# Routing-table entries loaded into registers four at a time instead of one by one

## The chip, the cores and the metric

The kernel runs on one core of one Trainium2 chip. The metric is the device time of one execution in microseconds (us); before the change it is 420.66 us, the median of three runs (418.88, 420.66 and 421.48). Engines are named as in the profile: PE (TensorE), DVE (VectorE), ACT (ScalarE), POOL (GpSimd) and SP (SyncE, which here only issues DMA transfers).

## The reference

One block of a vision transformer with a mixture of experts, in float32, on 32 images of 37 tokens of width 256 (1184 tokens):

```python
h = patches @ W.T + b + pos_embd                     # 36 patches an image, and a class token
h = h + attention(layernorm(h))                      # 16 heads, silu on q and k, rope, causal, gated
x = layernorm(h)
topidx = 6 of 32 experts, from 2 of 4 groups, by sigmoid(x @ gate.T) + bias
routed = sum over the 6 of  w_e * (silu(x @ w_gate[e]) * (x @ w_up[e])) @ w_down[e]     # hidden 128
shared = (silu(x @ sg) * (x @ su)) @ sd
anchor = the same form with 1 of 16 anchor experts, chosen by topidx[:, 0] // 2          # hidden 64
h = h + routed + shared + 0.1 * anchor
```

Which expert a token goes to is known only once the gate has been computed, on the chip.

## The kernel before, in words

The first half (up to about 195 us) embeds the patches, does attention tile by tile, normalises again, computes the gate and, per token, its place in each expert's list. POOL scatters every token's row (width, weights and target rows, 322 numbers) into lists in HBM (`rows_d`), one list an expert, seven copies a token.

The second half goes over 112 tiles of 128 rows of these lists, called visits here: 25 for the anchor experts (kind "A", `FIRST_ROUTED` = 25) and 87 for the routed ones, of kinds "F" (a full tile of one expert), "M" and "X" (tiles at the seams of the lists). The kinds stand fixed in the program. Which expert's weights a visit takes, and from which row on, depends on the data: DVE computes it as a table of four lines of integers in the first partition of `scratch`, one column a visit. Line 0 is the place of the expert's weights in the weight tile `W`, line 1 the first row in `rows_d`, line 2 the column with the expert's weight, line 3 the place of the sum tile. An engine that needs an entry loads it into a register (`entry`, line 319, a TENSOR_LOAD in its instruction queue) and uses the register in an address:

- SP, `load_rows` (lines 405 to 414): waits until the row buffer is free (six buffers), loads the row number (line 1), issues the transfer of 128 rows into `G`.
- ACT, `copy_up` (line 977): loads the weights' place (line 0) and copies the expert's up and gate weights to `UPW`; then copies the turned rows (`turned_copy`, line 985) and does the silu (`hidden_silu`, line 990).
- PE: for visit i it loads the weights' place of visit i-1 (line 0, `down_weights`), then multiplies the turned rows with the up weights (line 823), turns the rows of visit i+2 (line 812) and multiplies the hidden values of visit i-1 with its down weights (line 838).
- DVE, main loop: loads the column of visit i+2 (`columns`, line 2) and, where the tile is summed and not of kind "M", the sum tile's place (line 3), then forms the hidden product of visit i (line 1597), takes weights and target rows of visit i+2 (lines 1566 and 1574, or 1576 for kind "F"), and adds the result of visit i-1 to its sum tile (`accumulate`, line 1589).

So an anchored visit has two loads on DVE and one on each of SP, ACT and PE. All instruction streams are written out in full, in the order given; engines wait for each other through semaphores only. POOL sends finished tiles to HBM, and at the end (from about 374 us) SP reads the sums back and DVE adds them to `h`.

Of the kernel before, what the change touches and what calls it, by code (L numbers as in the profile page):

```python
# [24 lines left out]
P = 128  # L25
D = 256
# [30 lines left out]
ANCHOR_COLS = ANCHORS * ANCHOR_WX  # L57
# [24 lines left out]
GB = 6  # L82
# [3 lines left out]
def routed(i):  # L86
    return KINDS[i] != "A"
# [22 lines left out]


FIRST_ROUTED = ANCHOR_TILES
EARLY_COLS = 19482
TRI4 = 3 * LISTS
SMALL = TRI4 + 23
PIECES = [[(0, 4), (4, 8), (8, NT)]] * (CHOICES - 1) + [[(0, 4), (4, 7), (7, 9), (9, 10), (10, NT)]]
assert KINDS.count("F") == FULL and KINDS.count("M") == MIXED and KINDS.count("X") == EXTRAS
assert all(KINDS[:i].count("X") >= min(EXTRAS, INDEX[i] + 1) for i in range(XT) if KINDS[i] == "M")
assert FULL * D <= ANCHOR_COLS and XT <= P
LATE_PIECES = 10  # L120
BIG = 3.0e38

# [1 line left out]
def build(nc, pt, wt, posr, brow, wqkv, wo, wg1, wg2, lnwb, gwt, gbias, sgu, sd, wx,  # L124
          ident_c, cmask_c, turn_c, parity_c, cs_c, before_c, small_c, out):
    with ExitStack() as ctx:
# [187 lines left out]
        fin_ok, out_st = sem("fin_ok"), sem("out_st")  # L314
        block = ctx.enter_context(nc.Block())

        def entry(engine, q, i, top):

            return nc.values_load(table[0:1, q, bass.ds(i, 1)], engines=(engine,), min_val=0, max_val=top,  # L319
                                  skip_runtime_bounds_check_because="the table is computed within these bounds")  # L320

        def patch_view(b):

# [25 lines left out]
        def _(sp):  # L349
# [52 lines left out]
            sp.wait_ge(table_ok, 1)  # L402
            sp.wait_ge(av_ps, NT)

            def load_rows(i):
                if i == FIRST_ROUTED:
                    sp.wait_ge(scat, 16 * NT * TOPK)
                if i >= GB:

                    sp.wait_ge(T_ps, i - GB + 1)  # L410
                    sp.wait_ge(meta_ok, i - GB + 1)
                row = entry(mybir.EngineType.SP, 1, i, DUMMY_ROW + P)
                sp.dma_start(G[:, i % GB, :], rows_d[bass.ds(row, P), :]).then_inc(g_ld[i % GB], 16)

            def load_part(c):

# [85 lines left out]
        def _(pe):  # L502
# [301 lines left out]
            pe.wait_ge(table_ok, 1)  # L804
            pe.wait_ge(valid_ok, 1)
            pe.wait_ge(hs_ok, NB - 2)

            def turn_rows(i):

# [16 lines left out]

            def down_weights(i):
                size, at = (WX, UP_COLS) if routed(i) else (ANCHOR_WX, ANCHOR_UP_COLS)
                e = entry(mybir.EngineType.PE, 0, i, (W_COLS if routed(i) else ANCHOR_COLS) - size)
                return W[:, bass.ds(e, size)][:, at:at + D]  # L830

            def down(i, weights):
                if i == FIRST_ROUTED:
# [19 lines left out]
        def _(act):  # L853
# [120 lines left out]
            for b in range(3, NB):  # L974
                shared_silu(b)

            def copy_up(i):

                size, n = (WX, UP_COLS) if routed(i) else (ANCHOR_WX, ANCHOR_UP_COLS)
                e = entry(mybir.EngineType.Activation, 0, i, (W_COLS if routed(i) else ANCHOR_COLS) - size)  # L980
                act.copy(UPW[:, i % 2, 0:n], W[:, bass.ds(e, size)][:, 0:n]).then_inc(upw_ok, 1)  # L981

            def turned_copy(i):
                act.wait_ge(T_ps, i + 1)
# [31 lines left out]
        def _(dve):  # L1016
# [524 lines left out]
            dve.wait_ge(table_ok, 1)  # L1541
            dve.wait_ge(valid_ok, 1)

            def sum_tile(i):
                if KINDS[i] == "M":
                    k = INDEX[i] * RING
                    return mixed[:, k:k + D], mixed_rows[:, k + D:k + RING]
                top = (MIXED if routed(i) else ANCHOR_PACKED) * RING - RING
                k = entry(mybir.EngineType.DVE, 3, i, top)
                sums, rows = (mixed, mixed_rows) if routed(i) else (ring, ring_rows)  # L1550
                return sums[:, bass.ds(k, D)], rows[:, bass.ds(k + D, 1)]

# [1 line left out]

            def columns(i):

                at = entry(mybir.EngineType.DVE, 2, i, ALPHA_COL)
                if summed(i):
                    tiles[i] = sum_tile(i)
                return at  # L1560

            def take_columns(i, at):

                mask = valid[:, i:i + 1]
                dve.wait_ge(T_ps, i + 1)
                dve.tensor_tensor(wcol[:, i:i + 1], G[:, i % GB, bass.ds(at, 1)], mask, ALU.mult)  # L1566
                to = G[:, i % GB, TO_ROW:ROW][:, bass.ds(at, 1)]
                if summed(i):
                    if KINDS[i] != "A" and INDEX[i] == 0:
                        dve.wait_ge(mixed_zero, 2)  # L1570
                    if i > 0:
                        dve.wait_ge(meta_ok, i)
                    rows = tiles[i][1]
                    dve.scalar_tensor_tensor(rows, to, mask, rows, ALU.mult, ALU.add).then_inc(meta_ok, 1)  # L1574
                else:
                    dve.tensor_copy(tok_full[:, INDEX[i]:INDEX[i] + 1], to).then_inc(meta_ok, 1)
# [92 lines left out]
def constants():  # L1669
# [16 lines left out]
    small[:, 2 * LISTS:3 * LISTS] = P + np.arange(LISTS) * LIST_ROWS  # L1686
    small[:, TRI4:TRI4 + 16] = np.tril(np.ones((GROUPS, GROUPS)), -1).ravel()
    small[:, TRI4 + 16] = row
    number = np.array([number_of(i) if i < XT else -1 for i in row], np.float32)
    small[:, TRI4 + 17] = number  # L1690
    small[:, TRI4 + 18] = [0 if i >= XT or KINDS[i] == "X" else -P * number[i] for i in row]
    last = np.array([ANCHOR_PACKED - 1 if i < XT and KINDS[i] == "A" else MIXED - 1 for i in row], np.float32)
    small[:, TRI4 + 19] = [(number[i] if i < XT and KINDS[i] == "A" else 0) - last[i] for i in row]
    small[:, TRI4 + 21] = last
    small[:, TRI4 + 20] = SPARE_ROW + row
    small[:, TRI4 + 22] = [ANCHOR_COLS if i < XT and KINDS[i] != "A" else 0 for i in row]
    return dict(ident_c=np.eye(P, dtype=np.float32), cmask_c=causal, turn_c=turn, parity_c=parity, cs_c=cs.astype(np.float32),
                before_c=before, small_c=small)

# [16 lines left out]
```

## Time and profile before

| what | before |
|---|---|
| runs | 418.88, 420.66, 421.48 us; median 420.66 us |
| span of the profiled execution, first to last instruction | 412.1 us |
| time around the span, by the three runs | 6.8 to 9.4 us |
| PE busy | 343.3 us (83%) |
| DVE busy | 278.0 us (67%) |
| ACT busy | 190.0 us (46%) |
| POOL busy | 181.7 us (44%) |

The profile records one execution; its own time from outside is not given, its span is. Register, branch and semaphore instructions and the loads from the table do not count as busy: they show as waits put down to "issue", or in an engine's queue, which the views name DVEq, SPq, ACTq or PEldq (PEld is PE's weight load). "PEclk" is the clock granted to PE as a share of its full speed. The chain of waits is followed back from the last instruction to what released it.

### The profile page before, as it was taken

How to read it: one execution, taken by the hardware profiler on the slowest of the kernel's cores; microseconds unless marked ns; L12 is line 12 of the kernel's file. 1: busy time of each engine (PE TensorE's matmuls, PEld its weight loads, DVE VectorE, ACT ScalarE, POOL GpSimd, SP SyncE). 2: the span in 40 equal slices, each digit the busy share in tenths (PEclk: the TensorE clock that was granted, in tenths of full speed). 3: DMA queues.
4: the chain of work that ended last, by engine and by line, in shares of the span. 5: the costliest groups of instructions: out<-in, count | busy, mean ns of one | idle time of the engine just before them, and what ended most of it. 6: DMA issues, size and time to landing. Idle time of an engine off the chain costs nothing.

```text
span 412.1 us, 8817 instructions
## 1 busy us (share of the span) xinstructions
PE 343.3 (83%) x2552; PEld 299.1 (73%) x2552; DVE 278.0 (67%) x1171; ACT 190.0 (46%) x471; POOL 181.7 (44%) x159
## 2 busy tenths in 40 slices
PE   5999999999899968773889999999999999994000
PEld 3786978779687857561677789999999999993000
DVE  0466789989798886798357775555565665666675
ACT  1152153441545233400157777777877777771000
POOL 6000000588888768767871374344422344433000
PEclk9999999999999997985989999999999999998555
DMA  7999999986698643694555576555555559531998
GB/s 234 298 335 335 329 341 328 420 320 119 123 337 252 126 96 86 218 387 137 152 162 130 167 214 180 162 158 165 165 145 162 166 155 291 168 113 58 303 303 245
DMA packets 55823, 88.44 MB, mean 215 GB/s; under 512 B 16145, under 2 KB 46521, under 8 KB 55513
## 3 DMA queue, kind: packets, MB, share of 16 engines
q1 hardware_dynamic: 38192, 67.66, 52.9%
q0 software_dynamic: 16720, 19.48, 17.8%
q10 hardware_dynamic: 864, 0.73, 0.6%
q8 instruction: 21, 0.34, 0.3%
q14 instruction: 26, 0.21, 0.2%
HBM read 50.62 MB, written 37.09 MB: 213 GB/s over the span
## 4 chain that ended last, share of the span: by engine, by line
PE 60%; DVE 20%; DMA 8%; issue 3%; ACT 3%; SPq 3%; DVEq 2%; POOLq 0%
PE B L823 20%; PE B L838 10%; PE B L514 6%; PE B L812 5%; DMA W<-sums_d 4%; PE B L549 4%; PE B L632 3%; PE B L598 2%; PE B L618 2%; DVEq L319 2%; DMA e_sb<-rows_d 2%; SPq L419 2%; DVE ring L1589 1%; PE B L656 1%; DMA W<-in_pt 1%
## 5 line engine op out<-in xcount | busy, mean ns | idle before, releaser
L457 POOL DMA_INDIRECT rows_d<-spent,slot x77 | 104.1, 1352 | 97.3 <-issue 90.9
L823 PEld LDWEIGHTS B<-e_sb,UPW 128*128 128x128 f32 x796 | 105.4, 193 | 10.7 <-issue 5.5
L823 PE MATMUL B<-e_sb,UPW 128*128 128x128 f32 x796 | 108.9, 278 | 1.5 <-issue 1.5
L1597 DVE TENSOR_TENSOR e_sb<-e_sb,B 128x128 f32<-128x128 f32 (+1 forms) x112 | 32.3, 288 | 62.2 <-ACT e_sb L990 55.8
L981 ACT COPY UPW<-W 128x512 f32 (+1 forms) x112 | 63.9, 570 | 22.2 <-issue 13.9
L838 PE MATMUL B<-W,e_sb 128*128 x224 | 69.3, 391 | 0.8 <-DVE e_sb L1597 0.8
L483 POOL DMA_INDIRECT sums_d<-spent x32 | 31.1, 972 | 48.7 <-DVE spent L1589 47.9
L812 PE MATMUL B<-ident,e_sb 128*128 128x128 f32 x224 | 43.1, 274 | 1.9 <-DMA e_sb<-rows_d 1.8
L990 ACT ACTIVATE e_sb<-B 128x128 f32<-128x128 f32 (+1 forms) x112 | 30.9, 276 | 22.2 <-PE B L823 20.8
L514 PE MATMUL B<-W 128*111 128x256 f32 (+1 forms) x132 | 34.2, 406 | 4.6 <-DMA W<-in_pt 4.5
L483 POOL DMA_INDIRECT sums_d<-W,tok_full x24 | 23.2, 966 | 30.3 <-ACT W L995 29.7
L838 PEld LDWEIGHTS B<-W,e_sb 128*128 128x128 f32 x224 | 34.0, 192 | 3.5 <-issue 1.7
L985 ACT COPY e_sb<-B 128x256 f32<-128x256 f32 x88 | 32.3, 367 | 4.6 <-PE B L812 4.6
L514 PEld LDWEIGHTS B<-W 128*111 128x111 f32 (+1 forms) x132 | 23.3, 184 | 12.2 <-DMA W<-in_pt 5.3
L1589 DVE SCALAR_TENSOR_TENSOR spent<-B,wcol,spent 128x256 f32<-128x256 f32 (+1 forms) x63 | 30.4, 482 | 1.7 <-DVE spent L1574 0.8
L812 PEld LDWEIGHTS B<-ident,e_sb 128*128 128x128 f32 x224 | 28.5, 144 | 2.3 <-DMA e_sb<-rows_d 2.1
L1626 DVE TENSOR_TENSOR h<-h,W 112x1024 f32<-112x1024 f32 (+3 forms) x23 | 23.2, 1047 | 8.4 <-DMA W<-sums_d 8.4
L1289 DVE TENSOR_TENSOR e_sb<-B,spent 111x444 f32<-111x444 f32 (+1 forms) x44 | 23.6, 597 | 4.1 <-PE B L598 4.1
L1566 DVE TENSOR_TENSOR wcol<-e_sb,turn 128x1 f32<-128x1 f32 x112 | 17.2, 153 | 4.0 <-PE B L812 3.8
L598 PE MATMUL B<-W 32*111 32x222 f32 (+1 forms) x176 | 15.5, 369 | 4.8 <-ACT W L909 4.8
L549 PE MATMUL B<-W 128*128 128x222 f32 (+1 forms) x96 | 18.1, 341 | 0.6 <-ACT W L886 0.6
L606 PE MATMUL B<-spent 128*128 128x256 f32 x70 | 18.6, 414 | 0.0
(250 smaller groups left out, 524.0 us busy)
## 6 DMA issues: line engine op xcount, KB each, us to landing
e_sb<-rows_d SPq DMA_DIRECT2D x112, 161.0 KB, 2.3
rows_d<-spent SPq DMA_DIRECT2D x2, 7728.0 KB, 44.4
W<-in_wx SPq DMA_DIRECT2D x1, 6643.0 KB
W<-sums_d SPq DMA_DIRECT2D x13, 448.0 KB, 9.4
W<-in_wx SPq DMA_DIRECT2D x10, 516.5 KB, 9.5
W<-in_wx SPq DMA_DIRECT2D x1, 4576.0 KB, 18.7
W<-in_pt SPq DMA_DIRECT2D x4, 666.0 KB, 6.9
W<-sums_d SPq DMA_DIRECT2D x7, 336.0 KB, 11.1
```

The costliest lines, as they stand in the source:

```text
L457: pool.indirect_dma_start(rows_d, bass.IndirectOffsetOnAxis(ap=slot[0:n, t, j:j + 1], axis=0), xrow[0:n, t, :], None).then_inc(done, 16)
L483: pool.indirect_dma_start(sums_d, bass.IndirectOffsetOnAxis(ap=rows, axis=0), src, None).then_inc(done, 16)
L514: m = pe.matmul(B[0][0:TILES[t], i * D:(i + 1) * D], patch_view(b)[:, c, at:at + TILES[t]], w_patch[:, c, :], start=c == 0, stop=c == PC - 1)
L549: m = pe.matmul(B[4 + half][:, c * BT:c * BT + n], w_qkv[:, k, lo:lo + P], xnT[:, k, 0:n], start=k == 0, stop=k == KC - 1)
L812: m = pe.transpose(B[i % 2][:, k * P:(k + 1) * P], G[:, i % GB, k * P:(k + 1) * P], ident[:, :])
L823: mm = pe.matmul(B[2 + i % 2][:, m * P:(m + 1) * P], UPW[:, i % 2, at:at + P], GT[:, i % 2, k, :], start=k == 0, stop=k == KC - 1)
L838: pe.matmul(B[6 + i % 2][:, 0:D], hid[:, i % 2, :], weights, start=True, stop=True).then_inc(D_ps, 1)
L981: act.copy(UPW[:, i % 2, 0:n], W[:, bass.ds(e, size)][:, 0:n]).then_inc(upw_ok, 1)
L985: act.copy(GT[:, i % 2, :, :].rearrange("p k s -> p (k s)"), B[i % 2][:, 0:D]).then_inc(gt_by[True], 1)
L990: act.activation(S[0:n, i % 2, :], B[2 + i % 2][0:n, 0:P], ACT.Silu).then_inc(silu_ok, 1)
L1589: dve.scalar_tensor_tensor(sums, B[6 + i % 2][:, 0:D], wcol[:, i:i + 1], sums, ALU.mult, ALU.add).then_inc(acc_ok, 1)
L1597: dve.tensor_tensor(out[0:n, i % 2, :], S[0:n, i % 2, :], ups, ALU.mult).then_inc(H_ok, 1)
```

## The change

`entry` is replaced by `entries`: one load instruction fetches up to four neighbouring entries of a line into up to four registers, and a dictionary on each engine keeps them for the visits that follow. A group does not go beyond the anchored visits or the end, and starts where the column number is a multiple of four; for that, the routed visits' columns are moved to begin at column 28 in place of 25 (`place_of`), in the table, in the constants from which it is computed, and in the column of `valid`. On SP a group's load comes before the waits for the row buffer, in place of behind them.

```diff
--- before.py
+++ after.py
@@ -110,13 +110,20 @@
 FIRST_ROUTED = ANCHOR_TILES
+
+
+def place_of(i):
+
+    return i if i < FIRST_ROUTED else i - FIRST_ROUTED - (-FIRST_ROUTED // 4) * 4
+
+
 EARLY_COLS = 19482
 TRI4 = 3 * LISTS
 SMALL = TRI4 + 23
 PIECES = [[(0, 4), (4, 8), (8, NT)]] * (CHOICES - 1) + [[(0, 4), (4, 7), (7, 9), (9, 10), (10, NT)]]
 assert KINDS.count("F") == FULL and KINDS.count("M") == MIXED and KINDS.count("X") == EXTRAS
 assert all(KINDS[:i].count("X") >= min(EXTRAS, INDEX[i] + 1) for i in range(XT) if KINDS[i] == "M")
-assert FULL * D <= ANCHOR_COLS and XT <= P
+assert FULL * D <= ANCHOR_COLS and place_of(XT - 1) < P
 LATE_PIECES = 10
 BIG = 3.0e38
 
@@ -314,10 +321,17 @@
         fin_ok, out_st = sem("fin_ok"), sem("out_st")
         block = ctx.enter_context(nc.Block())
 
-        def entry(engine, q, i, top):
-
-            return nc.values_load(table[0:1, q, bass.ds(i, 1)], engines=(engine,), min_val=0, max_val=top,
-                                  skip_runtime_bounds_check_because="the table is computed within these bounds")
+        def entries(engine, q, i, top):
+
+            at = place_of(i)
+            n = 4 - at % 4
+            if i < FIRST_ROUTED:
+                n = min(n, FIRST_ROUTED - i)
+            n = min(n, XT - i)
+            _, found = nc.values_load_multi_w_load_instructions(
+                table[0:1, q, at:at + n], engines=(engine,), min_val=0, max_val=top,
+                skip_runtime_bounds_check_because="the table is computed within these bounds")
+            return {i + k: v for k, v in enumerate(found)}
 
         def patch_view(b):
 
@@ -402,15 +416,18 @@
             sp.wait_ge(table_ok, 1)
             sp.wait_ge(av_ps, NT)
 
+            row_of = {}
+
             def load_rows(i):
+                if i not in row_of:
+                    row_of.update(entries(mybir.EngineType.SP, 1, i, DUMMY_ROW + P))
                 if i == FIRST_ROUTED:
                     sp.wait_ge(scat, 16 * NT * TOPK)
                 if i >= GB:
 
                     sp.wait_ge(T_ps, i - GB + 1)
                     sp.wait_ge(meta_ok, i - GB + 1)
-                row = entry(mybir.EngineType.SP, 1, i, DUMMY_ROW + P)
-                sp.dma_start(G[:, i % GB, :], rows_d[bass.ds(row, P), :]).then_inc(g_ld[i % GB], 16)
+                sp.dma_start(G[:, i % GB, :], rows_d[bass.ds(row_of[i], P), :]).then_inc(g_ld[i % GB], 16)
 
             def load_part(c):
 
@@ -804,6 +821,7 @@
             pe.wait_ge(table_ok, 1)
             pe.wait_ge(valid_ok, 1)
             pe.wait_ge(hs_ok, NB - 2)
+            weights_of = {}
 
             def turn_rows(i):
 
@@ -826,8 +844,9 @@
 
             def down_weights(i):
                 size, at = (WX, UP_COLS) if routed(i) else (ANCHOR_WX, ANCHOR_UP_COLS)
-                e = entry(mybir.EngineType.PE, 0, i, (W_COLS if routed(i) else ANCHOR_COLS) - size)
-                return W[:, bass.ds(e, size)][:, at:at + D]
+                if i not in weights_of:
+                    weights_of.update(entries(mybir.EngineType.PE, 0, i, (W_COLS if routed(i) else ANCHOR_COLS) - size))
+                return W[:, bass.ds(weights_of[i], size)][:, at:at + D]
 
             def down(i, weights):
                 if i == FIRST_ROUTED:
@@ -974,11 +993,14 @@
             for b in range(3, NB):
                 shared_silu(b)
 
+            weights_of = {}
+
             def copy_up(i):
 
                 size, n = (WX, UP_COLS) if routed(i) else (ANCHOR_WX, ANCHOR_UP_COLS)
-                e = entry(mybir.EngineType.Activation, 0, i, (W_COLS if routed(i) else ANCHOR_COLS) - size)
-                act.copy(UPW[:, i % 2, 0:n], W[:, bass.ds(e, size)][:, 0:n]).then_inc(upw_ok, 1)
+                if i not in weights_of:
+                    weights_of.update(entries(mybir.EngineType.Activation, 0, i, (W_COLS if routed(i) else ANCHOR_COLS) - size))
+                act.copy(UPW[:, i % 2, 0:n], W[:, bass.ds(weights_of[i], size)][:, 0:n]).then_inc(upw_ok, 1)
 
             def turned_copy(i):
                 act.wait_ge(T_ps, i + 1)
@@ -1541,12 +1563,16 @@
             dve.wait_ge(table_ok, 1)
             dve.wait_ge(valid_ok, 1)
 
+            sum_at, column_at = {}, {}
+
             def sum_tile(i):
                 if KINDS[i] == "M":
                     k = INDEX[i] * RING
                     return mixed[:, k:k + D], mixed_rows[:, k + D:k + RING]
                 top = (MIXED if routed(i) else ANCHOR_PACKED) * RING - RING
-                k = entry(mybir.EngineType.DVE, 3, i, top)
+                if i not in sum_at:
+                    sum_at.update(entries(mybir.EngineType.DVE, 3, i, top))
+                k = sum_at[i]
                 sums, rows = (mixed, mixed_rows) if routed(i) else (ring, ring_rows)
                 return sums[:, bass.ds(k, D)], rows[:, bass.ds(k + D, 1)]
 
@@ -1554,14 +1580,15 @@
 
             def columns(i):
 
-                at = entry(mybir.EngineType.DVE, 2, i, ALPHA_COL)
+                if i not in column_at:
+                    column_at.update(entries(mybir.EngineType.DVE, 2, i, ALPHA_COL))
                 if summed(i):
                     tiles[i] = sum_tile(i)
-                return at
+                return column_at[i]
 
             def take_columns(i, at):
 
-                mask = valid[:, i:i + 1]
+                mask = valid[:, place_of(i):place_of(i) + 1]
                 dve.wait_ge(T_ps, i + 1)
                 dve.tensor_tensor(wcol[:, i:i + 1], G[:, i % GB, bass.ds(at, 1)], mask, ALU.mult)
                 to = G[:, i % GB, TO_ROW:ROW][:, bass.ds(at, 1)]
@@ -1686,14 +1713,16 @@
     small[:, 2 * LISTS:3 * LISTS] = P + np.arange(LISTS) * LIST_ROWS
     small[:, TRI4:TRI4 + 16] = np.tril(np.ones((GROUPS, GROUPS)), -1).ravel()
     small[:, TRI4 + 16] = row
-    number = np.array([number_of(i) if i < XT else -1 for i in row], np.float32)
-    small[:, TRI4 + 17] = number
-    small[:, TRI4 + 18] = [0 if i >= XT or KINDS[i] == "X" else -P * number[i] for i in row]
-    last = np.array([ANCHOR_PACKED - 1 if i < XT and KINDS[i] == "A" else MIXED - 1 for i in row], np.float32)
-    small[:, TRI4 + 19] = [(number[i] if i < XT and KINDS[i] == "A" else 0) - last[i] for i in row]
-    small[:, TRI4 + 21] = last
+    small[:, TRI4 + 17] = -1
+    for i in range(XT):
+        k, anchor = place_of(i), KINDS[i] == "A"
+        last = (ANCHOR_PACKED if anchor else MIXED) - 1
+        small[k, TRI4 + 17] = number_of(i)
+        small[k, TRI4 + 18] = 0 if KINDS[i] == "X" else -P * number_of(i)
+        small[k, TRI4 + 19] = (number_of(i) if anchor else 0) - last
+        small[k, TRI4 + 21] = last
+        small[k, TRI4 + 22] = 0 if anchor else ANCHOR_COLS
     small[:, TRI4 + 20] = SPARE_ROW + row
-    small[:, TRI4 + 22] = [ANCHOR_COLS if i < XT and KINDS[i] != "A" else 0 for i in row]
     return dict(ident_c=np.eye(P, dtype=np.float32), cmask_c=causal, turn_c=turn, parity_c=parity, cs_c=cs.astype(np.float32),
                 before_c=before, small_c=small)
 
```

Two places show what the engines execute. The first is the start of the visits on SP, where the rows of the first tiles are fetched; TENSOR_LOAD is the load from the table (`scratch`), ISA the register arithmetic of the address, DMA the transfer of 128 rows into `G` (which lies in `e_sb`). Before:

```order
L319 TENSOR_LOAD scratch [waits table_ok,av_ps,ini_d,scat_anchor]
L413 ISA
L413 DMA e_sb<-rows_d 128x322
L319 TENSOR_LOAD scratch
L413 ISA
L413 DMA e_sb<-rows_d 128x322
```

And now:

```order
L331 TENSOR_LOAD scratch [waits table_ok,av_ps,ini_d,scat_anchor]
L430 ISA
L430 DMA e_sb<-rows_d 128x322
L430 ISA
L430 DMA e_sb<-rows_d 128x322
L430 ISA
L430 DMA e_sb<-rows_d 128x322
```

One load now stands ahead of four transfers; the next follows ahead of the fifth.

The second place is an anchored visit on DVE: hidden product (before line 1597, now 1624), weight column (1566, now 1593), target rows (1574, now 1601), accumulation (1589, now 1616). Before, every visit begins with two loads:

```order
L319 TENSOR_LOAD scratch x2
L1597 TENSOR_TENSOR e_sb<-e_sb,B 64x128 [waits silu_ok]
L1566 ISA [waits T_ps]
L1566 TENSOR_TENSOR wcol<-e_sb,turn 128x1
L1574 ISA [waits meta_ok]
L1574 SCALAR_TENSOR_TENSOR ring<-e_sb,turn,ring 128x1
L1589 ISA [waits acc_ok,meta_ok,D_ps]
L1589 SCALAR_TENSOR_TENSOR ring<-B,wcol,ring 128x256
```

And now, from the first visit of a group into the second:

```order
L331 TENSOR_LOAD scratch x2
L1624 TENSOR_TENSOR e_sb<-e_sb,B 64x128 [waits silu_ok]
L1593 ISA [waits T_ps]
L1593 TENSOR_TENSOR wcol<-e_sb,turn 128x1
L1601 ISA [waits meta_ok]
L1601 SCALAR_TENSOR_TENSOR ring<-e_sb,turn,ring 128x1
L1616 ISA [waits acc_ok,meta_ok,D_ps]
L1616 SCALAR_TENSOR_TENSOR ring<-B,wcol,ring 128x256
L1624 TENSOR_TENSOR e_sb<-e_sb,B 64x128 [waits silu_ok]
```

The two loads stand before one product in four; the other three follow the accumulation directly. All other instructions and waits are as they were.

## Rows read from the trace of the kernel before

**Rows 1.** The page's first line: span and instructions.

```profile
span 412.1 us, 8817 instructions
```

**Rows 2.** Busy time by stretch: start:end, length, busy us (instructions) per engine, clock, DMA.

```profile
208.00:211.00 3.00, 2.99 (x12) 2.82 (x13) 1.48 (x7) 1.56 (x5) 3.00 (x2) 0.50 0.70 183
211.00:237.00 26.00, 25.77 (x164) 20.09 (x163) 19.87 (x78) 18.87 (x61) 8.56 (x6) 1.00 0.54 148
241.00:374.00 133.00, 133.00 (x1036) 128.59 (x1036) 77.64 (x347) 101.73 (x259) 55.00 (x57) 1.00 0.57 168
```

**Rows 3.** Chain of waits, routed visits: start us, us, what.

```profile
241.66 0.22 PE B L812 x2
241.87 0.43 PE B L838 x2
242.31 0.89 PE B L823 x8
...
371.95 0.89 PE B L823 x8
```

**Rows 4.** Timeline of DVE, an anchored visit: start us, us, instruction, [idle before].

```profile
223.79 0.29 DVE L1597 TENSOR_TENSOR e_sb<-e_sb,B 64x128 f32<-64x128 f32 x1 [0.21 <-issue]
...
224.38 0.48 DVE L1589 SCALAR_TENSOR_TENSOR ring<-B,wcol,ring 128x256 f32 x1
225.07 0.29 DVE L1597 TENSOR_TENSOR e_sb<-e_sb,B 64x128 f32<-64x128 f32 x1 [0.21 <-issue]
```

**Rows 5.** Chain of waits, the anchored visit after that one.

```profile
226.00 0.31 DVEq L319
```

**Rows 6.** Line 319, 213 to 412 us: duration ns min/median/max, first and last start.

```profile
L319 DVEq TENSOR_LOAD <-scratch x157: 297/308/540, 212.8 to 370.5; - x157
...
L319 SPq TENSOR_LOAD <-scratch x101: 262/268/712, 213.8 to 363.0; - x101
```

**Rows 7.** The same line, 195 to 211.5 us.

```profile
L319 SPq TENSOR_LOAD <-scratch x10: 267/799/1447, 195.3 to 210.6; - x10
L319 DVEq TENSOR_LOAD <-scratch x10: 308/721/1812, 201.5 to 211.0; - x10
```

**Rows 8.** Chain of waits, run-up to the visits.

```profile
194.49 0.69 DVE scratch L1530
...
195.34 1.30 SPq L319
...
196.85 0.36 SPq L413
...
197.24 1.07 SPq L319
...
198.48 6.87 DMA e_sb<-rows_d
...
206.54 1.47 issue
208.01 1.20 PE B L823 x4
...
211.89 0.10 DVE e_sb L1597
```

**Rows 9.** A routed visit on PE: its table load, and the weight load after it.

```profile
L319 PEldq TENSOR_LOAD <-scratch x1: 310/310/310, 301.1 to 301.1; - x1
...
302.12 0.19 PEld L823 LDWEIGHTS B<-e_sb,UPW 128*128 128x128 f32 x1
```

**Rows 10.** Timeline of DVE, an anchored visit with one load ahead of its second product.

```profile
238.27 0.29 DVE L1597 TENSOR_TENSOR e_sb<-e_sb,B 64x128 f32<-64x128 f32 x1 [0.22 <-issue]
...
238.85 0.48 DVE L1589 SCALAR_TENSOR_TENSOR ring<-B,wcol,ring 128x256 f32 x1
239.36 0.29 DVE L1597 TENSOR_TENSOR e_sb<-e_sb,B 64x128 f32<-64x128 f32 x1
```

**Rows 11.** DMA issues, 195 to 211 us: count, KB each, median us to landing.

```profile
e_sb<-rows_d SPq DMA_DIRECT2D x9, 161.0 KB, 6.2
```

## The prediction

> **What bounds the kernel now.** I read the stretches first [rows 1, 2]. The table from which the loads take their numbers is ready at about 195 us [rows 8] of a span of 412.1 us; what comes before does not execute a changed line. The 87 routed visits (241 to 374 us) come next: the reader sees TensorE (PE) busy 133.00 of 133.00 us at granted clock 1.00. In the chain of waits the same group of matmuls stands at 242.31 and, 84 visits later, at 371.95, so a visit takes 129.64 / 84 = 1.543 us [rows 3], which is its own eight, two and two passes: 0.89 + 0.22 + 0.43 = 1.54. No engine but PE can shorten that stretch. What is left is the 25 anchored visits (about 206 to 240 us) and the run-up to them.
>
> In the anchored stretch the timeline of VectorE (DVE) shows a visit every 1.28 us (hidden product at 223.79, the next at 225.07), and 0.21 us of idleness before each product, put down to "issue" [rows 4]. The chain says what that is: the second of the two table loads, 0.31 us in DVE's queue, after the accumulation and before the product [rows 5]. Nobody else is waited for. So here DVE's two loads per visit set the end.
>
> At the run-up the loads are not 0.31 us. After 213 us one takes 0.308 us on DVE and 0.268 on SP in the median; between 195 and 211.5 us it takes 0.80 on SyncE (SP) and 0.72 on DVE in the median and up to 1.8 [rows 6, 7]. The chain runs through SP's first load (1.30), the first row transfer's issue, SP's second load (1.07) and the second transfer (6.87), then through PE's 1.47 us of "issue" (its own first load) and a first-layer group of 1.20 us at granted clock 0.50 [rows 2, 8].
>
> **The change part by part.** Loads go from 112 to 29 on SP, PE and ScalarE (ACT), and from 168 to 58 on DVE; nothing is added, nothing else is reordered, except that SP and the others take a group's load at its first visit.
>
> *Routed visits: 0.* PE's load there is covered by queued matmuls: one starts at 301.1 and takes 0.31, and the next visit's first weight load comes only at 302.12 [rows 9], 0.7 us after its end. ACT is busy 101.73 and DVE 77.64 of 133 us [rows 2], so their loads stand beside PE as well. If a load of four took more than about 0.31 + 0.7 = 1.0 us, that cover would be gone and PE would stop once in four visits.
>
> *Anchored visits: -2.85.* Near the end of the stretch there is a visit that already has only one load, since the first routed tile needs no sum. There the product follows the accumulation's start by 239.36 - 238.85 = 0.51 us instead of 0.69, and the visit takes 239.36 - 238.27 = 1.09 us [rows 10]. The accumulation alone lasts 0.48, so one load hides beneath it, and a visit without any is no slower: 1.28 - 1.09 = 0.19 saved. After the change two loads stand before the products of visits 2, 6, 10, 14, 18 and 22, and none before the others. Between product 2 (211.89 [rows 8]) and product 22 (238.27 [rows 10]) there are twenty steps; fifteen lose their loads: 15 x 0.19 = 2.85. The other five stay at 1.28 if a load of four costs what a load of one does. What is late next: PE needs half of 0.89, plus 0.22 and 0.43, that is 1.095 us, for an anchored visit [rows 3], so it stands level with DVE and a further saving would find it there. ACT is busy 18.87 of 26 us [rows 2], below 1 us a visit, so it is not next.
>
> *The price of a load of four registers* is in no row. From below it is the load of one, 0.31; from above four of them, 4 x 0.308 = 1.23. I take 0.31: the register arithmetic and the move between SP's first load (ended 196.64) and its transfer (196.85) take 0.21 us together where the load took 1.30 [rows 8], so most of a load is its trip to memory, and four neighbouring words can share one; the load of one is also the nearest row. If the words were paid one by one, the loaded step would be 1.28 + 2 x (L - 0.31), and the four-visit group breaks even where 2 x (L - 0.31) = 3 x 0.19, at L = 0.595.
>
> A page speaks against my choice: the Trainium skill, "Runtime: NRT & Kernel Launch", section on instruction fetch mechanics, says that a register load costs about 200 ns for each register even in bulk, of loads from HBM. By that, as an estimate, L would be 0.31 + 0.6 = 0.91, the group 0.63 us longer than now, and the anchored part would lose 5 x 0.63 = 3.2 us where my sum gains 2.85. The trace has only loads of one word from on-chip memory, so no row shows which holds. Another page, "DMA: Bandwidth & Descriptors", section on latency and other measured facts, gives a load a floor of about 600 ns and says that unrolling by four amortizes it; the trace disagrees with the floor (0.26 to 0.31 us in most of it).
>
> *The run-up: -1.1.* SP's load before the second row transfer (1.07) goes, so that transfer is issued at about 197.4 instead of 198.48. I let its 6.87 us stand and move the whole chain by 1.1. Bounds: 0, if the transfer is slow because of what else the DMA engines do (the nine row transfers of this stretch take 6.2 us in the median [rows 11]) and lands at the old time anyway; and 1.1. PE's first load stays (1.47 on the chain). ACT's and DVE's loads that go here lie beside that one.
>
> *The clock: -0.3.* From 208 to 211 us the granted clock is 0.50 [rows 2], at which PE needs 2 x 1.095 = 2.19 us a visit; as long as it lasts, absent loads buy little. Coming 1.1 us earlier, the group that took 1.20 us [rows 8] falls into full clock, where four passes take 0.45 [rows 3], but the next ones still meet the low one. I take 0.3 of the difference. Bounds: +0.5 (the low stretch comes at a busier moment) to -1.5 (no low stretch at all: 3 us at half speed).
>
> *The end* (from 374 us) has no changed line and only moves up.
>
> Sum: -2.85 - 1.1 - 0.3 = -4.25 us. The trace gives a span of 412.1 us for one execution; the three runs shown are 418.88, 420.66 and 421.48, so 6.8 to 9.4 us lie around the span, which the change does not touch. Against the median: 420.66 - 4.25 = 416.4 us.
>
> **The rivals.**
>
> *Words are paid one by one (slower).* Place: the DVE queue in every fourth anchored visit, and SP's first load. For it: the run-up loads of 1.3 to 1.8 us show that a load's time is that of its trip [rows 7, 8], and four trips could follow each other. Against it: four neighbouring words, one instruction. At L = 1.23 the loaded step is 3.12, a group 3 x 1.09 + 3.12 = 6.39 in place of 5.12, over five groups +6.35; SP's first load becomes 4 x 1.30, and the second row is issued at about 201.1 instead of 198.48, +2.6: 429.6 us. At half of that (L = 0.77) the anchored part costs +1.75 and the run-up nothing: 422.4. It decides from L = 0.595 upward. Chance 0.11, time about 426.
>
> *The run-up gives nothing.* Rows land when the DMA engines let them, or the low clock stretches over what was won; only the 2.85 is left: 417.8. For it: 6.2 us a transfer there, and the 0.50. Chance 0.15.
>
> *A load of four costs 0.5 to 0.6.* The anchored gain is eaten (five times 0.4 to 0.57 off 2.85), the run-up stays: 418.5 to 419.3. Chance 0.10. The same time comes out if DVE, freed, only waits for PE.
>
> *The forecast.* 0.64, its own range 415.0 to 417.6.
>
> **How the numbers follow.** 1% of 420.66 is 4.2 us, about what a measurement of this kernel can tell from no change, and the forecast lies on that line. Within its 0.64 I put 0.62 on the faster side, since a clock that does not drop would add up to 1.5: 0.40 for faster by over 1%. Within 1%: 0.64 x 0.38 + 0.15 + 0.10 = 0.49. Slower by over 1%: 0.11. The range goes from 414.3 (the twenty steps all at 1.09, 3.8, and 2.6 from run-up and clock) up to 420.9, which takes in both cases without a sign of their own and leaves out the slow one.
>
> **What would show it.** Right: load rows of about 0.3 us after 213 us, 29 on PE; in DVE's timeline three anchored visits in four at 1.09 to 1.12 us with no "issue" before the product, every fourth at 1.28; the second row transfer issued 0.5 us after the first; routed visits still 1.543 apart. Wrong: load rows of 0.6 us or more; anchored visits unevenly long with a product waiting for the queue; the second row landing at 205.4 as before; a gap in PE's routed stretch every fourth visit. A low clock of another length in the run-up would move the total by up to 1.5 us without touching the argument on the loads.

## The result and the profile after

The changed kernel takes 412.63 us (median of 11 runs, 410.19 to 416.55); the kernel before, run beside it, 418.88 us (median of 11). The ratio is 0.9873, 95% interval 0.9839 to 0.9908; it is formed of the fast runs alone, those within 1.5% of the fastest of the same kernel in their batch, so here and below it need not be the quotient of the two medians. The kernel is 1.3% faster, where the chances had 0.40 for more than 1% and 0.49 for less, and the time lies 1.7 us below the range. Of the 3.8 us between forecast and result, 1.8 are the base: the median of three runs shown before was 420.66. The other 2.0 are gain: 4.25 us predicted, 6.25 between the two medians; by the ratio it is 5.3 (3.9 to 6.7).

The first line of the page after, to be held against [rows 1]:

```profile
span 409.7 us, 8458 instructions
```

The table loads after 213 us, by engine (count, ns min/median/max, first and last start); [rows 6] answers to it. A load of four takes 0.344 us on DVE where one word took 0.308, and 0.304 on SP where one took 0.268. So L, the prediction's name for the time of a load of four, is 0.34, and its upper bound of 1.23 is far off.

```profile
L331 DVEq TENSOR_LOAD <-scratch x54: 315/344/1146, 216.0 to 365.5; - x54
L331 PEldq TENSOR_LOAD <-scratch x28: 316/332/772, 213.9 to 368.0; - x28
L331 ACTq TENSOR_LOAD <-scratch x27: 288/311/754, 216.3 to 365.6; - x27
L331 SPq TENSOR_LOAD <-scratch x26: 280/304/952, 212.2 to 356.1; - x26
```

The anchored visits in DVE's timeline after (start, us, instruction, idle time before it); [rows 4] answers to it. The reader is to see the distance of the products: 1.04, 1.04, 1.24 and 1.10 us, which repeats. Three products follow the accumulation (0.48) directly, with no "issue" ahead of them. The one that follows the two loads comes 0.24 us late. The view puts that down to ACT, but ACT's silu had ended at 226.30; the second of DVE's loads starts at 226.17 and takes 0.34, so it ends at 226.51, just ahead of the product. The loads are what it waits for.

```profile
223.24 0.29 DVE L1624 TENSOR_TENSOR e_sb<-e_sb,B 64x128 f32<-64x128 f32 x1
224.28 0.29 DVE L1624 TENSOR_TENSOR e_sb<-e_sb,B 64x128 f32<-64x128 f32 x1
225.32 0.29 DVE L1624 TENSOR_TENSOR e_sb<-e_sb,B 64x128 f32<-64x128 f32 x1
225.84 0.48 DVE L1616 SCALAR_TENSOR_TENSOR ring<-B,wcol,ring 128x256 f32 x1
226.56 0.29 DVE L1624 TENSOR_TENSOR e_sb<-e_sb,B 64x128 f32<-64x128 f32 x1 [0.24 <-ACT e_sb L1012]
227.66 0.29 DVE L1624 TENSOR_TENSOR e_sb<-e_sb,B 64x128 f32<-64x128 f32 x1
```

The chain of waits over the same visits (start, us, what) no longer has a DVE piece or a load in it, where [rows 5] had DVE's load at every visit. It is PE alone, without a gap: 0.44 + 0.22 + 0.43 = 1.09 a visit.

```profile
225.55 0.44 PE B L841 x4
225.99 0.22 PE B L830 x2
226.21 0.43 PE B L857 x2
226.64 0.44 PE B L841 x4
```

The windows (length, then busy us and instructions of PE, PEld, DVE, ACT, POOL, the granted clock, DMA share, GB/s) stand beside [rows 2]. They do not tell who sets the pace: in the anchored stretch PE is busy 19.15 of 19.40 us, and it was busy 25.77 of 26.00 when DVE's loads set it. What rose is DVE's share, from 19.87 of 26.00 to 16.40 of 19.40. The routed stretch is unchanged, PE 132.91 of 133.00. And from 208 to 211 us the granted clock is 1.00 where the profile before had 0.50.

```profile
208.00:211.00 3.00, 2.68 (x19) 2.45 (x19) 2.24 (x11) 1.91 (x8) 3.00 (x2) 1.00 0.59 155
216.60:236.00 19.40, 19.15 (x135) 17.46 (x136) 16.40 (x66) 14.21 (x50) 8.05 (x6) 1.00 0.60 160
239.00:372.00 133.00, 132.91 (x1032) 128.09 (x1030) 77.12 (x345) 95.86 (x259) 55.23 (x57) 1.00 0.58 169
```

A routed visit in the chain after, beside [rows 3]: from one group of eight to the next is 241.17 - 239.62 = 1.55, and over 84 visits the mean is 1.543, as before.

```profile
239.62 0.89 PE B L841 x8
...
241.17 0.89 PE B L841 x8
```

The run-up is where little can be read from one execution. Loads between 195 and 211.5 us after, beside [rows 7]: fewer; DVE's are longer in the median (0.99 against 0.72), SP's shorter (0.49 against 0.80).

```profile
L331 DVEq TENSOR_LOAD <-scratch x4: 350/986/2885, 202.4 to 209.6; - x4
L331 SPq TENSOR_LOAD <-scratch x3: 447/493/1271, 195.8 to 209.1; - x3
L331 PEldq TENSOR_LOAD <-scratch x1: 1051/1051/1051, 205.9 to 205.9; - x1
```

The chain of waits there, beside [rows 8]: DVE's first pair of loads takes 2.88 + 1.57 us, holds back the first weight columns, with them the release of the row buffers, and so SP's next transfers, issued at 207.72, 208.74 and 209.81. PE waits for the first of these until 213.64, 1.85 us (the second view), and for the third until 216.62. The first wait is why the profiled execution shows one anchored step of 3.28 us (212.18 to 215.46) without a counterpart before.

```profile
202.43 2.88 DVEq L331
...
205.34 1.57 DVEq L331
...
207.72 0.33 SPq L430
...
209.81 6.76 DMA e_sb<-rows_d
216.57 0.04 issue
216.62 0.44 PE B L830 x2
```

```profile
213.64 0.44 PE L830 MATMUL B<-ident,e_sb 128*128 128x128 f32 x2 [1.85 <-DMA e_sb<-rows_d]
```

### The profile page after: what moved, and what is told of

Its sections match the earlier page's. It is cut to its first block, busy times and chain, and to the rows that moved or that the text cites. A ratio compares the mean times of both kernels' runs of the same rounds, so it can differ in the third digit from the quotient of the medians.

```text
span 409.7 us, 8458 instructions
## 1 busy us (share of the span) xinstructions
PE 338.0 (83%) x2552; PEld 297.7 (73%) x2552; DVE 277.1 (68%) x1171; ACT 182.0 (44%) x471; POOL 183.4 (45%) x159
## 4 chain that ended last, share of the span: by engine, by line
PE 62%; DVE 19%; DMA 9%; SPq 3%; ACT 3%; issue 2%; DVEq 1%; POOLq 0%
PE B L841 21%; PE B L857 11%; PE B L830 6%; PE B L531 5%; DMA W<-sums_d 4%; PE B L566 3%; PE B L649 2%; PE B L615 2%; DMA W<-in_wg 2%; PE B L720 2%; DMA e_sb<-rows_d 2%; SPq L436 2%; PE B L635 1%; PE B L623 1%; DVE stats L1057 1%
## 5 line engine op out<-in xcount | busy, mean ns | idle before, releaser
L474 POOL DMA_INDIRECT rows_d<-spent,slot x77 | 105.4, 1369 | 96.7 <-issue 95.7
L841 PE MATMUL B<-e_sb,UPW 128*128 128x128 f32 x796 | 107.2, 275 | 0.9 <-ACT e_sb L1007 0.7
L857 PE MATMUL B<-W,e_sb 128*128 x224 | 67.2, 382 | 0.7 <-DVE e_sb L1624 0.7
L500 POOL DMA_INDIRECT sums_d<-W,tok_full x24 | 23.3, 969 | 30.0 <-ACT W L1017 29.4
L531 PEld LDWEIGHTS B<-W 128*111 128x111 f32 (+1 forms) x132 | 22.7, 180 | 12.4 <-DMA W<-in_pt 5.9
L1653 DVE TENSOR_TENSOR h<-h,W 112x1024 f32<-112x1024 f32 (+3 forms) x23 | 23.2, 1047 | 8.8 <-DMA W<-sums_d 8.8
```

The lines of the kernel that those rows point to most:

```text
L474: pool.indirect_dma_start(rows_d, bass.IndirectOffsetOnAxis(ap=slot[0:n, t, j:j + 1], axis=0), xrow[0:n, t, :], None).then_inc(done, 16)
L500: pool.indirect_dma_start(sums_d, bass.IndirectOffsetOnAxis(ap=rows, axis=0), src, None).then_inc(done, 16)
L531: m = pe.matmul(B[0][0:TILES[t], i * D:(i + 1) * D], patch_view(b)[:, c, at:at + TILES[t]], w_patch[:, c, :], start=c == 0, stop=c == PC - 1)
L841: mm = pe.matmul(B[2 + i % 2][:, m * P:(m + 1) * P], UPW[:, i % 2, at:at + P], GT[:, i % 2, k, :], start=k == 0, stop=k == KC - 1)
L857: pe.matmul(B[6 + i % 2][:, 0:D], hid[:, i % 2, :], weights, start=True, stop=True).then_inc(D_ps, 1)
```

## The experiments

Every kernel below is the changed one with a width for each engine in place of the fixed 4, and ran beside the kernel before:

```
-            n = 4 - at % 4
+            width = WIDTH[engine]
+            n = width - at % width
```

Where SP loads one by one, its load stands behind the waits for the row buffer, as in the kernel before.

A measure used for all of them: the time from hidden product 9 to 22 (13 anchored steps, clear of the run-up), read from DVE's timeline as in [rows 4]. Before: 17.04 us. The whole change: 15.27 in the profile above and 14.75, 14.87 and 15.61 in the executions of three later batches.

**Which engine's loads count.** WIDTH is 4 on DVE and 1 elsewhere:

> Only VectorE loads four entries at a time; SyncE, TensorE and ScalarE load one each visit, as before. Theory A (VectorE's two loads set the pace of the anchored visits, as predicted): the anchored visits fall from 1.28 to about 1.10 us and the kernel gains 2.9 to 3.5 us, most of the whole change. Theory B (the whole change's 1.3% comes mostly from the run-up, where loads on every engine take 0.3 to 1.8 us beside the scatters, so fewer loads on any engine help): this kernel gains under 2 us.

Only SP by four:

> Only SyncE loads four at a time. Theory A: the second row's transfer is issued about 0.5 us after the first and the kernel gains about 1 us, the anchored visits stay at 1.28. Theory B: about 1 us as well. If it gains nothing, the first rows' landing does not depend on their issue.

All but DVE by four:

> SyncE, TensorE and ScalarE load four at a time, VectorE one each, two loads a visit, as before. Theory A: the anchored visits stay at 1.28 us and only the run-up moves, by 1 to 1.5 us. Theory B: 2.5 to 4 us are gained, since 27 of the run-up's 28 slow loads fall to about 13 without VectorE's help.

And the whole change beside them:

> The whole change once more, for its ratio on this chip and a second profile. Both theories: 0.984 to 0.991 of the time before. The loads of four at about 0.33 us, anchored visits 1.10 us on average. Theory A expects the run-up (from the table to the fourth hidden product) to differ between profiles of the same kernel by 1 to 4 us; theory B expects it to be shorter than before's in each.

Measured: DVE alone 0.9901 (0.986 to 0.9942), the whole change 0.986 (0.9811 to 0.9908); SP alone 1.001 (0.9967 to 1.0053), all but DVE 1.0041 (0.9998 to 1.0085). The 13 steps take 15.43 us with DVE alone and 14.75 with the whole change, 17.04 with SP alone and 17.03 with all but DVE. So most of the gain is DVE's loads in the anchored visits, and the other engines' 249 fewer loads give nothing while DVE's stay. The chain of the DVE kernel shows PE in the anchored stretch although PE still loads one word for each visit:

```profile
226.88 0.44 PE B L842 x4
...
227.97 0.45 PE B L842 x4
```

**What a load of several words costs.** First groups of two on all engines (WIDTH 2):

> Entries loaded two at a time on all four engines. In the changed kernel an anchored step without loads takes VectorE 1.04 us, one with two loads 1.24, and four of them 1.10 a step on average, which is also TensorE's need of 1.095. Theory A (VectorE with fewer loads is faster than TensorE, so TensorE sets the anchored pace): here every second step has loads, (1.04 + 1.24) / 2 = 1.14, so VectorE sets it again at 1.14 and the kernel lies 0.8 to 1 us behind groups of four. Theory of the prediction (steps of 1.09 without and 1.28 with loads): 1.19 a step, 1.7 us behind. A load of two should take about 0.32 us if each further word costs 12 ns.

Then groups of eight (WIDTH 8):

> Entries loaded eight at a time on all four engines. If a further word costs about 12 ns, a load of eight takes 0.39 to 0.40 us on VectorE. Theory A (TensorE sets the anchored pace): steps stay at 1.10 on average and the kernel is level with groups of four within 0.7 us. If VectorE's loads still set it, a step falls to about 1.07 and 0.6 us more is gained. If words beyond a 16-byte piece cost a trip of their own, the load takes about 0.6 us.

Measured: two, 1.0023 (0.9992 to 1.0055), no gain at all; eight, 0.9941 (0.9905 to 0.9978). The first missed, since a load of two costs far more than a load of four; the load of eight is the 0.6 us of the last case of its expectation. DVE's row of two, and behind it that of eight:

```profile
L333 DVEq TENSOR_LOAD <-scratch x97: 307/534/860, 214.0 to 373.8; - x97
```

```profile
L333 DVEq TENSOR_LOAD <-scratch x30: 315/602/1924, 216.0 to 366.6; - x30
```

With two, the 13 steps take 16.48 us, 0.56 less than before: most of what one load in place of two saves, its longer time gives back. That is not DVE's doing alone. In the chain PE stands alone, but every second group of four takes 0.66 in place of 0.44: PE's own load of two starts at 227.46 and lasts 0.53, and the weight load of that group comes only at 228.12, after 0.35 of "issue". So in an anchored visit PE's queued matmuls cover a load of 0.34 to within 0.1 us (behind it, in the profile after, the group takes 0.46 and 0.53), and not one of 0.53.

```profile
227.08 0.44 PE B L843 x4
...
228.18 0.66 PE B L843 x4
```

With eight, the 13 steps take 15.29 us. DVE's dear step, 1.72, comes once in eight there, and some visits behind it the products stand 1.10 apart without any load, where DVE alone takes 1.04; the chain over them is PE alone. That is PE's pace:

```profile
231.32 0.29 DVE L1626 TENSOR_TENSOR e_sb<-e_sb,B 64x128 f32<-64x128 f32 x1
...
232.42 0.29 DVE L1626 TENSOR_TENSOR e_sb<-e_sb,B 64x128 f32<-64x128 f32 x1
...
233.51 0.29 DVE L1626 TENSOR_TENSOR e_sb<-e_sb,B 64x128 f32<-64x128 f32 x1
```

From product 22 to 111 the kernel with eight takes 137.01 us where the whole change takes 136.09, so it loses a little in the routed visits; by what was not followed.

Then the change itself with every entry moved up two places in the table, so that each four lies across a 16-byte boundary:

```
-    return i if i < FIRST_ROUTED else ...
+    return 2 + (i if i < FIRST_ROUTED else ...)
...
+            n = width - (at - 2) % width
```

> The whole change, with every entry of the table moved up by two places, so that a group of four starts eight bytes off a 16-byte boundary and lies across it. Theory A (four neighbouring words cost one trip because they lie in one aligned piece of 16 bytes; across its edge two trips are paid): a load of four after 213 us takes about as much as the load of two or of eight, 0.53 to 0.60 us on DVE in place of 0.344; the loaded anchored step goes from 1.24 to 1.6 to 1.75, which the three unloaded ones at 1.04 give back only in part (1.65 + 3 x 1.04 = 4.77 against 4 x 1.095 = 4.38 a group), so about 5 x 0.4 = 2 us of the gain go: ratio to before 0.991 to 0.995. Theory B (it is the number of words, four, that makes the load short, and not where they lie): 0.344 and a ratio of 0.985 to 0.989, as after.

Measured: 436.52 us, ratio 1.0431 (1.0372 to 1.049). Where the words lie decides, so theory B fell; theory A had the direction but was far short in size. Its load takes not two but four trips' worth: 0.965 us on DVE, that is 0.308 and three times 0.219.

```profile
L333 DVEq TENSOR_LOAD <-scratch x40: 535/966/1193, 255.5 to 383.8; - x40
L333 PEldq TENSOR_LOAD <-scratch x19: 998/1003/1253, 259.5 to 378.9; - x19
```

In the kernel after, three groups on DVE near the end hold three words, and take 0.75, one such step less:

```profile
L331 DVEq TENSOR_LOAD <-scratch x3: 753/755/815, 360.1 to 365.5; - x3
```

So on DVE one, two and three words take 0.31, 0.53 and 0.75 us and four across the boundary 0.97: 0.22 more for each word. Four that fill an aligned 16 bytes take 0.34, and eight aligned ones 0.60. The rival of words paid one by one has its order right wherever the words do not fill an aligned 16 bytes, at 0.22 for each further word and not the 0.31 of its upper price; for those that do, it was wrong. Of starts off the boundary, only the one by two words was run with a whole group.

The shifted kernel also shows what the prediction said of PE's cover. At a load of 1.00 us PE stops once in four routed visits, in the chain as 0.14 of "issue" and a group of 1.13 in place of 0.89, 0.38 together; the routed visits come to 1.66 us in the mean, 0.12 more, of which this is 0.095. From product 22 to 111 that adds 10.7 us (146.81 against 136.09), and the 13 anchored steps take 20.99 against 14.75.

```profile
291.87 0.89 PE B L843 x8
...
299.97 0.14 issue
300.11 1.13 PE B L843 x8
```

**Whether PE's own loads count once DVE is freed.** DVE and PE by four, twice:

> DVE and PE load by four, SP and ACT one for each visit. Theory A (DVE's loads alone carry the gain): the same as DVE alone, ratio 0.986 to 0.991. Rival (freed of its loads, DVE finds PE as the next in the anchored stretch, and PE's own loads by four then give something that they don't give while DVE is late): 0.980 to 0.986, with anchored steps nearer to 1.06 than to 1.10.

> DVE and PE by four, SP and ACT one by one, a second time, to bound what SP's groups give in the run-up (the term of 1.1 us). Theory C, if SP's second load is the one that counted: 1 to 2 us behind the whole change. Theory D: the same as the whole change within 0.8 us.

The whole change beside them:

> The whole change once more, as the measure for the other three. Both theories: ratio 0.984 to 0.990.

> The whole change, as the measure for the other three on this chip. Both theories: ratio 0.983 to 0.990.

Measured: DVE and PE 0.9883 (0.9826 to 0.9941) and 0.9941 (0.9902 to 0.9981); the whole change 0.981 (0.973 to 0.9889) and 0.9916 (0.9877 to 0.9955). The 13 steps take 14.77 and 14.74 us, at the lower end of what the whole change takes (14.75 to 15.61), and the steady steps are 1.10, as with DVE alone (15.43 in its one profile), not the 1.06 of the rival. So PE's groups add nothing that these times can show, and the rival is not borne out. What SP's and ACT's add is less clear: by the ratios DVE and PE lie 3.1 and 1.0 us behind the whole change on the two chips, where theory C wanted 1 to 2; by the medians they lie 0.6 ahead and 1.1 behind, and the intervals overlap.

**Whether the run-up gave anything.** The first four visits alone by groups, and the reverse:

```
-            width = WIDTH[engine]
+            width = 4 if i < 4 else 1      (the reverse: i >= 4)
```

> Only the loads of the first four visits are grouped by four, on all four engines; every later visit loads its entries one by one, as before. Theory C (some 1 to 2 us of the gain lie in the run-up, where a load takes 0.7 to 1.8 us and visits 1 to 3 each paid for theirs): 1 to 2.5 us faster than before, ratio 0.994 to 0.998. Theory D (the run-up gives nothing, because the row transfers or the low clock decide there): ratio 0.998 to 1.002.

> The other half: the first four visits load their entries one by one, all later ones by four. Theory C: the anchored saving alone, 16 of the 20 steps at 1.10 in place of 1.28 and the odd 0.15 of the routed part, about 3.1 us, ratio 0.991 to 0.994, and 1.5 to 3 us behind the whole change. Theory D: within 1 us of the whole change, ratio 0.985 to 0.991.

Measured: first four alone 0.9945 (0.9902 to 0.9987), all but them 0.9924 (0.9892 to 0.9956), the whole change on this chip 0.9916. The first speaks for theory C, 2.3 us by its ratio, with an interval from 0.5 to 4.1. All but the first four matches C's sum of 3.1 us (0.0076 of 418.69 is 3.2) and lies just above D's range, but the whole change is only 0.3 us better by the ratios, where C wanted 1.5 to 3; that speaks for D. The traces do not carry C either. From the table's readiness to product 9, before takes 26.06 us, SP alone and all but DVE 24.68 and 26.91, and the kernel with only the first four grouped 27.57. In the chain of the latter the second transfer starts 0.55 after the first (198.87, 199.42), as the change intends, and the loads and the issuing of transfers that follow have become the longer pieces:

```profile
196.94 1.73 SPq L333
...
202.93 2.62 SPq L333
...
206.65 1.91 SPq L434
...
209.59 7.47 DMA e_sb<-rows_d
```

This stays open: a share of 0 to 2 us in the run-up is neither shown nor excluded.

**Moving the first loads ahead.** Since DVE's and PE's first loads stand on the run-up's chain, they were issued earlier, PE's ahead of its first transposes, DVE's pair ahead of two accumulations of the shared part:

```
+            first = down_weights(0)
             turn_rows(0)
...
             shared_mult(5)
+            dve.wait_ge(table_ok, 1)
+            sum_at = entries(mybir.EngineType.DVE, 3, 0, ANCHOR_PACKED * RING - RING)
+            column_at = entries(mybir.EngineType.DVE, 2, 0, ALPHA_COL)
             shared_add(4)
```

PE's alone, then both, and both again:

> The changed kernel with TensorE's first group load moved ahead of the first turned tile, where TensorE only waits for rows. If the first load (1.05 and 2.29 us in the two profiles of the changed kernel) stands on the path of the run-up, 0.5 to 2 us less than the changed kernel; if the rows or VectorE are late anyway, no difference beyond 0.3 us.

> As the one before, and VectorE's first two group loads also moved up, right behind its last product for TensorE's shared experts and ahead of the last two additions. If the first hidden product waits for these loads (2.9 + 1.6 us and 0.9 + 1.7 us in the two profiles), another 0.5 to 2 us less; if the rows land later than they end, no difference.

> The whole change with PE's first load ahead of its first transposes and DVE's first pair ahead of two accumulations of the shared part, beside the plain change on the same chip. Theory (the first loads, 1 to 3 us long in the run-up, stand on the path to the first anchored visits): faster than the plain change by 0.5 to 2 us, ratio to before 0.979 to 0.984. Rival (the first visits wait for the row transfers, and the loads lie beside that): the same as the plain change within 0.3 of a per cent.

Measured: PE's alone 414.71 us, 0.9931 (0.9897 to 0.9966); both 412.49 and 412.53 us, 0.9791 (0.9728 to 0.9855) and 0.9888 (0.9824 to 0.9951). From the table to product 9, PE's alone takes 23.2 us and both 22.7 and 23.3; four executions of the whole change take 23.2, 24.4, 24.9 and 27.5. To product 22 the three take 38.0 to 38.2, the four 38.8 to 42.4. The traces thus lean towards a shorter run-up; the times do not decide. PE's alone has the weakest ratio of the three, and beside the whole change on the same chip both together have the weaker ratio and the lower median (0.9888 against 0.981, the intervals overlap; 412.53 us against 414.51). That this version beats the change is not shown. In the chain of the repeat, from 196 to 212 us, no load of DVE or PE is left; two row transfers hold most of it:

```profile
196.75 7.28 DMA e_sb<-rows_d
...
208.15 6.28 DMA e_sb<-rows_d
```

## Why the prediction was right in direction and short in size

- **In short.** The mechanism of the main term was right. Two sizes failed: the anchored term, put at 2.85 us and measured at 3.7, and the base, 420.66, which lay 1.8 us above the 418.88 of the kernel run beside the change. With that base the range would have begun at 412.5.
- **What bounds the kernel.** Right. Taking DVE's two loads out of three anchored visits in four is what gave most of the gain; the routed visits stayed at 1.543.
- **Anchored visits, -2.85: the mis-sized term.** The step without a load was read as 1.09 from [rows 10], but that visit stands right behind a loaded product: its accumulation starts 238.85 - 238.27 = 0.58 us after its product, where in the kernel after, in a visit with no load just ahead of it, it is 225.84 - 225.32 = 0.52, and the step 1.04. The loaded step is 1.24 and not 1.28. So a group takes DVE 1.04 + 1.04 + 1.24 + 1.10 = 4.42 us, level with PE's 4 x 1.095 = 4.38, and the dear step is made up in the others: all twenty steps come to 1.10 in the mean, 20 x (1.284 - 1.10) = 3.7 us, where the sum left five at 1.28. From product 3 to product 22 the trace before takes 25.10 us and the whole change, in the execution of the second batch, where no row came late, 21.37: 3.73 less in 19 steps; in that of the third it is 21.58. In the other two executions late rows lengthen it, to 24.32 and 24.59. The prediction had named PE as next at 1.095, but put all twenty at 1.09 only into the range's lower end.
- **The price, 0.31.** Nearly right, 0.344, but by the layout and not by the argument: that neighbouring words share one trip fails for two words (0.53) and for a shifted four (0.97), and holds for the aligned fours that `place_of` sets up. The prediction did not name the alignment, and so far its price was luck. The sentence of the Trainium skill that spoke against it, "Runtime: NRT & Kernel Launch", section on instruction fetch mechanics (about 200 ns for each register even in bulk), agrees with the 0.22 of each further word and not with the aligned four, 0.012 a word.
- **The break-even of the slow rival.** Its formula prices a long load too low. At 0.965 its formula gives 3 x 1.09 + 1.28 + 2 x 0.655 = 5.86 us for four steps; the shifted kernel takes 6.3 to 6.7. In its chain (below) the loads of DVE are followed by PE and ACT one after the other, and the formula had DVE alone.

The chain of one loaded step of the shifted kernel, DVE's second load, its product, PE and ACT:

```profile
230.11 0.96 DVEq L333
231.08 0.05 issue
231.12 0.30 DVE e_sb L1626
231.43 0.13 issue
231.56 0.69 PE B L859 x2
232.25 0.46 PE B L843 x4
...
232.90 0.39 ACT UPW L1005
```

- **Run-up, -1.1.** Not borne out as it was told. In the profile after the second transfer starts 0.55 us after the first, as forecast, but it takes 7.45 us where the sum let 6.87 stand. It lands at 205.25, against 205.35 before; counted from SP's first load (195.78 and 195.34) that is 0.5 sooner, not 1.1. And SP by four alone is worth nothing in time (1.001), the lower bound of the term and the rival "the run-up gives nothing".
- **The clock, -0.3.** Not tied to the loads in a way that these runs show. A low stretch, some 3 to 7 us at clock 0.50 between 207 and 217 us, stands in three of three executions with DVE loading one word throughout, in all three with DVE by four and SP one by one, in two of four of the whole change, and in none of three with earlier first loads; the two kernels that group only the first four visits or only the others had none either.
- **What lies around the span.** Misread. In all later executions, those of the kernel before among them, time less span is 1.8 to 2.0 us (411.54 at 409.7 in the profile after), not 6.8 to 9.4. If that held for the profiled execution before as well, it took about 413.9 us, less than any of the 11 runs beside the change, and its rows are those of a quick execution. The sum was made in differences, so the forecast does not change by this, but its base, the median of three runs, was 1.8 us high.
- **What adds up.** Four batches of the whole change, weighted by their intervals, give 0.988 (plus or minus 0.002), 5.0 us. The anchored steps give 3.7 and the stretch from product 22 to 111 another 0.15 (136.24 to 136.09). Some 1.2 us are left (0.3 to 2.1 by that interval), and are the run-up's open share. That this comes near the 1.4 of the terms for run-up and clock is luck as far as these runs go, since neither path shows in them.

## What to carry to other kernels

When the limiting engine loses a cost in three steps of four, ask whether it is quicker than the next engine in the free steps: if it is, the dear step is made up there, and the next engine's pace prices all four. A price that rests on "neighbouring" needs its layout beside it; here the same four words cost 0.34 or 0.97 us by where they start. And a base that is the median of three runs can lie 2 us off when single executions spread by 6.

## What the runs showed of the hardware

- The time of a register load from the on-chip table goes by words except for aligned fours: 0.308, 0.534, 0.753 for one to three, 0.344 for four in an aligned 16 bytes, 0.965 for four across the boundary, 0.602 for eight aligned (DVE, medians). An aligned load of four is cheaper than a load of two.
- While the scatters on POOL's queue and the row transfers run, between 195 and 211.5 us, the same loads of the kernel after take from 0.35 to 2.9 us, and loads of four across the boundary up to 4.6 (SP in the shifted kernel, at 205.2 us). That the traffic stretches them is not shown apart.

```profile
L333 SPq TENSOR_LOAD <-scratch x2: 2874/3716/4557, 199.9 to 205.2; - x2
```

- A load runs in its engine's own queue, and what it costs depends on the work queued there: on DVE two loads of 0.31 us made the anchored step 1.28 us in place of 1.04; on PE a load of 0.34 costs an anchored visit less than 0.1, one of 0.53 delays its group by 0.22, and one of 1.00 stops PE in a routed visit.
